# The opening of a banded attention: order of the parts and row sums, queue of the first maxima, place of the block scales

## The chip, the cores and the metric

One of the cores of a Trainium2 chip runs the whole program. The metric is the device time of one execution in microseconds, taken over several runs.

## The reference, cut to what matters

Four layers are added to a stream x of 16 batches x 128 rows x 512 columns (float32): an attention over the columns within a band of 64, a feed-forward net whose three weights go through a 4-bit round trip (NF4), a cross attention, and a mixture of experts. The change touches only the time in which the first of them runs, and with it the round trip of the feed-forward weights, which is computed beside it.

```
x = x + _L0_xattn_ref(_layernorm(x), ctx_2048, ...)   # band |i - j| <= 64, 8 heads of 16
x = x + _L0_ffn_ref(_layernorm(x), weight1, weight2, weight3)
# nf4 round trip of each weight, in blocks of 64 values:
scalers_1 = max(abs(blocks), axis=1); scaler_mean = scalers_1.mean()
centered = scalers_1 - scaler_mean; sb = centered.reshape(nsb, 64)
qf = 256 / (2 * max(abs(sb), axis=1)); q_scalers = clip(round(sb * qf), -128, 127)
idx = argmin(abs(blocks / scalers_1 - NF4)); w = NF4[idx] * (q_scalers / qf + scaler_mean)
```

## The kernel before, in words

`phase_layer0_attention` is written out by hand: each engine has its own program, and semaphores tie them together. A batch is one 128 x 512 tile of x. It is normalised (`norm_x`), multiplied by the query and key weights (`proj`, TensorE, into two PSUM banks), and each product is split into three bf16 parts that add up to the float32 value: `first_part` and `second_part` on ScalarE, `resid_part` and `third_part` on VectorE. The parts have one SBUF buffer for all batches. SyncE writes it to DRAM (`write_parts`, L245) and loads it back in another order as the stacks `q_stack` and `k_stack` (`load_stack`, L253; twelve transfers for a batch, six for each half of the heads), which have two buffers. `first_part` of a later batch therefore waits until the write of the earlier one has landed.

The scores are computed twice. A first pass (`smax`, L508) gives the products of a half of the heads, in eight chunks, whose row maxima VectorE takes with the band mask (`take_max`, L777). The maxima are turned by TensorE (`max_t`, L514), split into two bf16 parts (`max_parts`, L789 and L791), written to DRAM and loaded back as two more rows of `q_stack` (`max_out` and `max_back`, L257 and L261, on SyncE). The second pass (`scores`, L523 and L528) then includes them, so that ScalarE can take the exponential directly (`exps`, L386). For the very first half (batch 0, first heads) GpSimd does this write and read, L334 and L336, with semaphores of their own; the scores of batch 0 wait for `s_mr0`. The two PSUM banks of the first pass alternate, and one of them also takes the turned maxima: from the second round on, TensorE's sixth chunk waits for `max_parts`.

```
def max_out(b, g, u):
    sp.wait_ge(s_mp, 2 * u + 2)
    sp.dma_start(dr_max[2 * b + g]..., mparts[:]).then_inc(s_mw, 16)
...
if c == MT_AT + 2:
    pe.wait_ge(s_mp, 4 * i + 6)
smax(2 * i + 3, 1 - b, 1, c)
```

In the main loop (`batches`; batches 0, 1 and the last two are written out, the others are a hardware loop) a batch has two rounds of eight chunks c. In each chunk TensorE does one first-pass chunk of the next half, one second-pass chunk of this half, a piece of the summing of the quantised weights (`nf4_sum`, L574), and here and there a product with the attention's values (`pv`, L540), a turn of outputs (L548, L554), a projection. VectorE does the maxima of a chunk and between them the pieces of the NF4 round trip.

The round trip needs block scales. For weight 1 the absolute maxima of the blocks of 64 are taken in the opening (L876), for weights 2 and 3 from magnitudes that ScalarE computes during batch 0 (`magnitudes`, `block_max`). GpSimd writes them to DRAM and reads them in another order (`gather_maxima`, L311 and L314); VectorE sums them and takes reciprocals (`block_sums`, `block_recip`, L850, L844, L845), TensorE forms the mean (L583), VectorE computes the scales in eleven dependent steps (`block_mean` L855, `block_scales`, L863 to L873), and GpSimd writes and reads them once more (`spread_scales`, L318 and L322). `nf4_weight` (L919) needs them: for the first two chunks of the weights those of weight 1, from the third on those of weights 2 and 3 as well. That third chunk is at the start of batch 2, the first turn of the hardware loop.

GpSimd's queue holds, in this order: load of weight 1, three loads of x, the gathering for weight 1, the first maxima's write and read, a wait for the first half of batch 1's stacks (`s_ld[0]` at 192), the loads of weights 2 and 3 (L306), the spreading of weight 1's scales. ScalarE's opening holds the parts of batch 0 (L364, L368), a root for two batches, four row sums (`row_sum`, L414: batches 4 to 7), the parts of batch 1, eight more row sums, twelve square sums (L419), the root of all of them (L440), then the main loop with the normalising of batch 2 (L373).

Of the kernel before, what the change touches and what calls it, by code (L numbers as in the profile page):

```python
# [25 lines left out]
NB, S, D = 16, 128, 512  # L26
# [50 lines left out]
def phase_layer0_attention(nc, T, I):  # L77
# [13 lines left out]
    DVE_ROWS = 4  # L91
# [15 lines left out]
    qst = sb("q_stack", [P, 2, H0, D], BF16)  # L107
# [3 lines left out]
    mparts = sb("max_parts", [16, 2, P], BF16)  # L111
# [41 lines left out]
    dr_max = nc.dram_tensor("dr_max", [4, 2, 16, P], BF16).ap()  # L153
# [73 lines left out]
    with nc.Block() as block:  # L227

        @block.sync
        def _(sp):  # L230
# [34 lines left out]
            for i in range(2):  # L265
                write_parts(i, i)
                for g in range(2):
                    load_stack(i, i, g, 16)
            def body(j, i, b, first, last, final):
                max_out(b, 1, 2 * i + 1)  # L270
                max_back(b, 1, 2 * i + 1)
                ge(sp, s_y, i - 1)
                sp.dma_start(ctx_sb[:, b, :], I["ctx"][bass.ds(i, 1), :, :].rearrange("o p d -> p (o d)")).then_inc(s_ctx[b], 16)
                if not last:
                    write_parts(i + 2, b)
                if not last:
                    sp.wait_ge(s_s, 16 * i + 8)
                    load_stack(i + 2, b, 0, 8 * (i - b) + 32)
                if not final:
                    max_out(1 - b, 0, 2 * i + 2)  # L280
                    max_back(1 - b, 0, 2 * i + 2)
                if not last:
                    sp.wait_ge(s_s, 16 * i + 16)
                    load_stack(i + 2, b, 1, 8 * (i - b) + 32)
# [4 lines left out]
        def _(pool):  # L289
# [40 lines left out]
            pool.memset(kst[96:98].rearrange("p a h t -> p (a h t)").bitcast(F32), TWO_ONES).then_inc(s_ko, 1)  # L330
            pool.wait_ge(s_am, 1)
            gather_maxima(0, 1)
            pool.wait_ge(s_mp, 2)
            pool.dma_start(dr_max[0].rearrange("c a t -> a c t"), mparts[:]).then_inc(s_mw0, 16)  # L334
            pool.wait_ge(s_mw0, 16)
            pool.dma_start(qst[96:98, 0, 0:4, :], dr_max[0].rearrange("c (h q) t -> c h (q t)", h=4)).then_inc(s_mr0, 16)  # L336
            pool.wait_ge(s_ld[0], 192)
            load_nf(1)
            load_nf(2)
# [8 lines left out]
        def _(act):  # L348
# [74 lines left out]
            for k in range(2):  # L423
                second_part(0, k)
            root(2, DVE_ROWS)
            for b in range(DVE_ROWS, DVE_ROWS + 4):
                row_sum(b)
            for k in range(2):
                first_part(1, 1, k)
            for k in range(2):  # L430
                second_part(1, k)
            for b in range(DVE_ROWS + 4, NB):
                row_sum(b)
            act.wait_ge(s_rs1, NSUM)
            act.activation(negmean[:, DVE_ROWS:NB], rsum[:, DVE_ROWS:NB], ACT.Copy, scale=-1.0 / D).then_inc(s_rs1, 1)
# [279 lines left out]
        def _(dve):  # L715
# [209 lines left out]
            def body(j, i, b, first, last, final):  # L925
                second = isinstance(i, int) and i == 1
                for c in range(8):
                    if not final:
                        take_max(2 * i + 2, 0, c)
                    if c in (3, 4) and not last:  # L930
                        resid_part(i + 2, c - 3)
                    if c == MT_AT:
                        max_parts(2 * i + 1, MT)
                    if c == 5 and not final:
                        v_copy(i + 1, 1 - b)
                    if c == 7 and first:
                        block_max(0)
                    if c == 5 and first:
                        block_scales(0, 1)
                    if c == 5 and second:  # L940
                        block_sums(1, 3)
                        block_recip(1, 3)
                    if c in (6, 7) and not last:
                        third_part(i + 2, c - 6)
                    if c == 7 and not first:
                        o_norm(i - 1, 1)
                    if c == 0:
                        if not first:
                            nf4_weight(2 * i - 2)
                    nf4_compare(2 * i, 0, c)  # L950
                    if c == 2:
                        nf4_scale(2 * i + 1, 1)
                for c in range(8):
                    if not final:
                        take_max(2 * i + 3, 1, c)
                        if c == MT_AT:
                            max_parts(2 * i + 2, MT)
                    if c == 2 and second:
                        block_mean(1, 3)
                    if c == 3 and second:  # L960
                        block_scales(1, 3)
                    if c in (1, 4, 7) and first:
                        block_max(1 + c // 3)
                    if c == 6 and not first:
                        gated(i - 1, 1 - b)
                    if c == 7:
                        o_norm(i, 0)
                    if c == 0:
                        if not first:
                            nf4_weight(2 * i - 1)  # L970
                    nf4_compare(2 * i + 1, 1, c)
                    if c == 2:
                        nf4_scale(2 * i + 2, 0)
                if first:
                    row_scale(2, DVE_ROWS, NB)
                if not first:
                    add_x(i - 1)
# [1929 lines left out]
```

## Time and profile before

| | us |
|---|---|
| three runs, median (lowest to highest) | 1455.07 (1453.42 to 1456.38) |
| profiled execution, its own time | 1452.38 |
| span of that execution | 1450.6 |
| start of the first scores product | 45.2 |

Times in the rows are microseconds from the span's start. "PE" is TensorE, "DVE" VectorE, "ACT" ScalarE, "POOL" GpSimd, "SPq" the issuing of SyncE. In the timeline a row gives start, duration, engine, line, operation, output and inputs, and in brackets the idle time of the engine before it with what ended it. L508 is line 508 of the program.

### The profile page before, as it was taken

To read this page: it belongs to the slowest core of one execution; us is meant where nothing else is said; L and a number is where in the kernel's file an instruction comes from. 1 tells how busy PE (TensorE), PEld (TensorE's weight loads), DVE (VectorE), ACT (ScalarE), POOL (GpSimd) and SP (SyncE) were. 2 spreads that over 40 slices of the span, in tenths; PEclk is the share of its full clock that TensorE was granted. 3 is DMA by queue.
4 is the path that set the end of the run, shared out by engine and by line. 5 is a ranking of instruction groups with operands and counts; after the bars stand their busy time and mean duration, and the time that the engine had idled before them with its cause. 6 is when DMAs were issued, how large, how long until landed. Compare 5 with 4: busy or idle time off the path is not lost. (4 is left out here: it accounts for less than half of the span.)

```text
span 1450.6 us, 28759 instructions
## 1 busy us (share of the span) xinstructions
PE 1355.9 (93%) x8732; PEld 818.1 (56%) x8732; DVE 977.6 (67%) x3234; ACT 788.2 (54%) x1802; POOL 245.7 (17%) x265
## 2 busy tenths in 40 slices
PE   3688999999999899999989999998788999999998
PEld 1345656565555444444455555555434877777774
DVE  6988999999996545546456788777568655444211
ACT  4877888888878533332367666667420233333231
POOL 3100000000000100000011000013311255555452
PEclk7799999999999999999999999999999999999999
DMA  8634353434430400000020000000413588898885
GB/s 258 172 79 99 81 123 96 117 95 111 108 82 10 146 0 0 0 0 1 0 76 15 16 16 14 14 0 31 151 70 111 165 259 251 246 255 251 243 243 116
DMA packets 63186, 149.52 MB, mean 103 GB/s; under 512 B 10792, under 2 KB 27830, under 8 KB 58892
## 3 DMA queue, kind: packets, MB, share of 16 engines
q1 hardware_dynamic: 49836, 115.70, 26.4%
q0 software_dynamic: 13280, 32.93, 9.9%
q8 instruction: 38, 0.62, 0.2%
q14 instruction: 32, 0.26, 0.1%
HBM read 113.21 MB, written 35.39 MB: 102 GB/s over the span
## 5 line engine op out<-in xcount | busy, mean ns | idle before, releaser
L777 DVE CUSTOM_DVE_ANT_0 masked_scores<-ps_max,band_mask 128x192 bf16<-128x192 f32 (+1 forms) x512 | 176.7, 382 | 17.7 <-PE ps_max L508 12.8
L386 ACT ACTIVATE probs_t<-ps_sc 128x448 f32<-128x448 f32 x256 | 139.1, 544 | 67.8 <-PE ps_sc L528 67.7
L1256 PE MATMUL f_ps<-f_xt,w_t 128*128 (+1 forms) x704 | 160.2, 382 | 2.5 <-ACT w_t L1311 2.5
L380 ACT ACTIVATE nf_above<-nf_scaled,nf_sign_at 128x512 f16<-128x512 bf16 x231 | 161.9, 717 | 0.0
L2804 DVE TENSOR_TENSOR d_inter<-d_silu_g,d_su 128x384 f32<-128x384 f32 x32 | 17.7, 554 | 161.7 <-PE d_su L2488 156.4
L1928 ACT ACTIVATE c_probs<-d_sg,c_negmax 128x128 f32<-128x128 f32 x256 | 90.3, 365 | 58.3 <-DVE c_negmax L2013 57.9
L508 PE MATMUL ps_max<-k_stack,q_stack 96*128 96x192 bf16 (+1 forms) x512 | 95.9, 271 | 26.7 <-DMA k_stack<-dr_parts 12.7
L1256 PEld LDWEIGHTS f_ps<-f_xt,w_t 128*128 128x128 bf16 x704 | 69.3, 98 | 86.7 <-issue 4.9
L2321 POOL DMA_INDIRECT out<-d_h,d_scatter_now x64 | 97.3, 1520 | 107.2 <-DMA out<-d_h,d_scatter_now 90.4
L2672 DVE TENSOR_SCALAR d_onehot<-d_slot_no,d_pos 128x192 bf16<-128x192 bf16 x512 | 101.0, 288 | 0.3 <-PE d_lb L2389 0.3
L508 PEld LDWEIGHTS ps_max<-k_stack,q_stack 96*128 96x128 bf16 x512 | 45.7, 100 | 93.8 <-issue 64.0
L2482 PE MATMUL d_su<-d_h,d_wgu 128*128 128x192 f32 x512 | 93.8, 338 | 1.4 <-DVE d_h L2791 1.1
L523 PE MATMUL ps_sc<-band_mask,identb 128*128 128x448 bf16 x256 | 92.0, 359 | 1.7 <-ACT probs_t L386 1.7
L528 PE MATMUL ps_sc<-q_stack,k_stack 98*128 98x192 bf16 (+1 forms) x512 | 92.5, 262 | 0.0
L2482 PEld LDWEIGHTS d_su<-d_h,d_wgu 128*128 128x128 f32 x512 | 84.5, 194 | 9.8 <-issue 9.8
L2488 PE MATMUL d_su<-d_h,d_wgu 128*128 128x192 f32 x512 | 88.7, 326 | 0.8 <-issue 0.8
L2488 PEld LDWEIGHTS d_su<-d_h,d_wgu 128*128 128x128 f32 x512 | 84.0, 190 | 1.1 <-issue 1.1
L1430 DVE SCALAR_TENSOR_TENSOR f_h<-f_ps,f_h_scale,f_silu 128x512 f32<-128x512 f32 x44 | 32.9, 749 | 76.7 <-PE f_ps L1256 76.6
L2013 DVE TENSOR_REDUCE c_negmax<-d_sg 128x4 f32<-128x512 f32 x64 | 44.1, 688 | 50.7 <-PE d_sg L1706 50.0
L1337 ACT ACTIVATE f_hparts<-f_h 128x512 f16<-128x512 f32 x44 | 27.7, 630 | 86.5 <-DVE f_h L1430 86.5
L2587 ACT ACTIVATE d_h<-d_sg 128x384 f32<-128x384 f32 (+1 forms) x32 | 14.0, 437 | 98.4 <-PE d_sg L2469 56.6
L528 PEld LDWEIGHTS ps_sc<-q_stack,k_stack 98*128 98x128 bf16 x512 | 50.9, 99 | 27.7 <-issue 2.2
(385 smaller groups left out, 2869.3 us busy)
## 6 DMA issues: line engine op xcount, KB each, us to landing
d_wgu<-in_ex_gu SPq DMA_DIRECT2D x32, 1024.0 KB, 6.9
d_wdown<-in_ex_d SPq DMA_DIRECT2D x32, 512.0 KB, 6.1
dr_parts<-qk_parts SPq DMA_DIRECT2D x32, 384.0 KB, 4.9
q_stack<-dr_parts SPq DMA_DIRECT2D x32, 192.0 KB, 2.8
k_stack<-dr_parts SPq DMA_DIRECT2D x32, 192.0 KB, 3.4
out<-x_sb SPq DMA_DIRECT2D x21, 256.0 KB, 2.1
nf_w<-in_nf_w POOLq DMA_DIRECT2D x3, 1408.0 KB, 9.3
q_stack<-dr_parts SPq DMA_DIRECT2D x32, 128.0 KB, 2.4
```

What stands on the lines that cost most here:

```text
L380: act.activation(above[:, g, k, :], lvl[:, g, :], ACT.Sign, bias=cut[:, k - NDV:k - NDV + 1]).then_inc(s_sg, 1)
L386: act.activation(pt[:, c, :], SP[c % 2][:].rearrange("p a w -> p (a w)")[:, a:z], ACT.Exp, scale=D0 ** -0.5).then_inc(s_e, 1)
L508: mm = pe.matmul(m[:, k, off:off + hi - lo], qst[0:96, b, h, qt * P:qt * P + P], kst[0:96, b, h, lo:hi], start=True, stop=True)
L523: pe.matmul(s[:].rearrange("p a w -> p (a w)")[:, a:z], identb[:], mask[:].rearrange("p a w -> p (a w)")[:, a:z], start=True, stop=False)
L528: mm = pe.matmul(s[:, k, off:off + hi - lo], kst[0:98, b, h, kt * P:(kt + 1) * P], qst[0:98, b, h, lo:hi], start=False, stop=(k == 1))
L777: op = dve.tensor_tensor_reduce(masked[:, c % 2, k, off:off + hi - lo], M[c % 2][:, k, off:off + hi - lo], mask[:, k, off:off + hi - lo], ...
L1256: mm = pe.matmul(bank[:], w12[:, m, kt, ft * P:(ft + 1) * P], xt[:, q, kt, bass.ds(g * N, N)], start=(kt == 0 and q == 0), stop=(kt == KT ...
L1928: op = act.activation(pr[:, ot % 2, j, :], SB[ot % 2][:, j, :], ACT.Exp, bias=nm[:, ot % 2, j:j + 1], accum_out=sm[:, bb, 4 * ot + j:4 * o ...
L2321: pool.indirect_dma_start(out, bass.IndirectOffsetOnAxis(ap=sst[rows_of[a], par, a:a + 1], axis=0), yo[a][:, par, :], None, compute_op=ALU ...
L2482: mm = pe.matmul(GP[:, it, :], wg[:, par, t, it * P:(it + 1) * P], xt[:, par, t, :], start=(t == 0), stop=(t == KT - 1))
L2488: mm = pe.matmul(UP[:, it, :], wg[:, par, t, FI + it * P:FI + (it + 1) * P], xt[:, par, t, :], start=(t == 0), stop=(t == KT - 1))
L2672: op = dve.tensor_scalar(oh[:, half, tl, jj, :], ios[:], pos[:, half * HT + tl, bass.ds(4 * q + jj, 1)], None, ALU.is_equal)
```

## The change

ScalarE's opening: the parts of batch 1 come ahead of all twelve row sums, where four of them stood ahead before. The first maxima are written and read by SyncE, behind the twelve issues of batch 1's stacks, and no longer by GpSimd; the semaphores are the same. In batch 1's rounds, VectorE's sums and reciprocals for weights 2 and 3 move from chunk 5 to chunk 4 of the first round, and the scales of these weights from chunk 3 to chunk 2 of the second round, where they follow the mean directly.

```diff
--- before.py
+++ after.py
@@ -266,6 +266,11 @@
                 write_parts(i, i)
                 for g in range(2):
                     load_stack(i, i, g, 16)
+            sp.wait_ge(s_mp, 2)
+            sp.dma_start(dr_max[0].rearrange("c a t -> a c t"), mparts[:]).then_inc(s_mw0, 16)
+            sp.wait_ge(s_mw0, 16)
+            sp.dma_start(qst[96:98, 0, 0:4, :], dr_max[0].rearrange("c (h q) t -> c h (q t)", h=4)).then_inc(s_mr0, 16)
+
             def body(j, i, b, first, last, final):
                 max_out(b, 1, 2 * i + 1)
                 max_back(b, 1, 2 * i + 1)
@@ -330,10 +335,6 @@
             pool.memset(kst[96:98].rearrange("p a h t -> p (a h t)").bitcast(F32), TWO_ONES).then_inc(s_ko, 1)
             pool.wait_ge(s_am, 1)
             gather_maxima(0, 1)
-            pool.wait_ge(s_mp, 2)
-            pool.dma_start(dr_max[0].rearrange("c a t -> a c t"), mparts[:]).then_inc(s_mw0, 16)
-            pool.wait_ge(s_mw0, 16)
-            pool.dma_start(qst[96:98, 0, 0:4, :], dr_max[0].rearrange("c (h q) t -> c h (q t)", h=4)).then_inc(s_mr0, 16)
             pool.wait_ge(s_ld[0], 192)
             load_nf(1)
             load_nf(2)
@@ -423,13 +424,11 @@
             for k in range(2):
                 second_part(0, k)
             root(2, DVE_ROWS)
-            for b in range(DVE_ROWS, DVE_ROWS + 4):
-                row_sum(b)
             for k in range(2):
                 first_part(1, 1, k)
             for k in range(2):
                 second_part(1, k)
-            for b in range(DVE_ROWS + 4, NB):
+            for b in range(DVE_ROWS, NB):
                 row_sum(b)
             act.wait_ge(s_rs1, NSUM)
             act.activation(negmean[:, DVE_ROWS:NB], rsum[:, DVE_ROWS:NB], ACT.Copy, scale=-1.0 / D).then_inc(s_rs1, 1)
@@ -937,7 +936,7 @@
                         block_max(0)
                     if c == 5 and first:
                         block_scales(0, 1)
-                    if c == 5 and second:
+                    if c == 4 and second:
                         block_sums(1, 3)
                         block_recip(1, 3)
                     if c in (6, 7) and not last:
@@ -957,7 +956,7 @@
                             max_parts(2 * i + 2, MT)
                     if c == 2 and second:
                         block_mean(1, 3)
-                    if c == 3 and second:
+                    if c == 2 and second:
                         block_scales(1, 3)
                     if c in (1, 4, 7) and first:
                         block_max(1 + c // 3)
```

## Rows read from the trace of the kernel before

**Rows 1.** The profile's page: busy time, share of the span and instructions of each engine.

```profile
PE 1355.9 (93%) x8732; PEld 818.1 (56%) x8732; DVE 977.6 (67%) x3234; ACT 788.2 (54%) x1802; POOL 245.7 (17%) x265
```

**Rows 2.** The timeline of all engines, the opening up to 40 us.

```profile
16.91 0.63 ACT L414 ACTIVATE unread<-x_sb 128x512 bf16<-128x512 f32 x1 [3.14 <-DMA x_sb<-in_x]
...
25.25 1.26 ACT L364 ACTIVATE qk_parts<-ps_g,bias 128x512 bf16<-128x512 f32 x2 [5.78 <-DMA dr_parts<-qk_parts]
...
30.68 0.90 PE L508 MATMUL ps_max<-k_stack,q_stack 96*128 96x192 bf16 x4 [12.74 <-DMA k_stack<-dr_parts]
...
38.49 0.56 POOL L334 DMA_DIRECT2D dr_max<-max_parts  x1 [11.80 <-DVE max_parts L791]
...
39.13 1.35 SPq L253 DMA_DIRECT2D k_stack<-dr_parts  x3
```

**Rows 3.** The timeline of all engines, 40 to 62 us.

```profile
41.81 0.30 ACT L440 ACTIVATE std<-square_sum,eps 128x12 f32<-128x12 f32 x1
...
42.99 1.90 POOL L306 DMA_DIRECT2D nf_w<-in_nf_w  x2
...
45.11 1.28 ACT L386 ACT_TABLE_LOAD   x1
45.23 0.58 PE L523 MATMUL ps_sc<-band_mask,identb 128*128 128x448 bf16 x1
...
49.66 0.42 DVE L777 CUSTOM_DVE_ANT_0 masked_scores<-ps_max,band_mask 128x256 bf16<-128x256 f32 x1 [1.31 <-PE ps_max L508]
```

**Rows 4.** The timeline of TensorE, 60 to 132 us.

```profile
60.47 0.48 PE L508 MATMUL ps_max<-k_stack,q_stack 96*128 96x192 bf16 x2 [3.50 <-DVE row_max L777]
...
97.02 0.32 PE L508 MATMUL ps_max<-k_stack,q_stack 96*128 96x192 bf16 x2 [0.89 <-DVE row_max L777]
...
105.17 0.38 PE L508 MATMUL ps_max<-k_stack,q_stack 96*128 96x256 bf16 x2
...
109.61 0.39 PE L508 MATMUL ps_max<-k_stack,q_stack 96*128 96x256 bf16 x2 [2.35 <-DVE row_max L777]
...
113.38 0.35 PE L523 MATMUL ps_sc<-band_mask,identb 128*128 128x448 bf16 x1
...
118.98 0.59 PE L574 MATMUL ps_nf<-nf_above,ident_f 128*128 128x512 f16 x2 [1.89 <-DVE nf_w L919]
```

**Rows 5.** The timeline of VectorE, 86 to 122 us.

```profile
94.08 0.40 DVE L850 TENSOR_REDUCE sc_sums<-sc_blocks 88x2 f32<-88x256 bf16 x1
...
94.67 1.25 DVE L845 RECIPROCAL absmax_recip<-absmax_recip 128x176 f32<-128x176 f32 x1
...
102.52 0.15 DVE L855 TENSOR_SCALAR sc_mean<-ps_g 128x2 bf16<-128x2 f32 x1
...
104.79 0.40 DVE L863 TENSOR_TENSOR sc_bf<-sc_blocks,sc_mean 88x256 bf16<-88x256 bf16 x1
...
108.17 0.42 DVE L873 TENSOR_TENSOR sc_bf<-sc_bf,sc_mean 88x256 bf16<-88x256 bf16 x1
...
118.14 0.69 DVE L919 SCALAR_TENSOR_TENSOR nf_w<-ps_nf,block_scale 128x512 f32 x1 [2.32 <-DMA block_scale<-dr_rep]
```

**Rows 6.** Groups by line, 0 to 60 us: busy us, mean ns, idle before.

```profile
L414 ACT ACTIVATE unread<-x_sb 128x512 bf16<-128x512 f32 x12 | 7.4, 615 | 3.1 <-DMA x_sb<-in_x 3.1
```

**Rows 7.** DMA issues, 0 to 60 us: queue, count, KB each, median us to landing.

```profile
sc_blocks<-dr_sc POOLq DMA_DIRECT2D x1, 22.0 KB, 5.0
...
dr_max<-max_parts POOLq DMA_DIRECT2D x1, 8.0 KB, 3.7
q_stack<-dr_max POOLq DMA_DIRECT2D x1, 8.0 KB, 2.0
dr_max<-max_parts SPq DMA_DIRECT2D x1, 8.0 KB, 2.8
```

**Rows 8.** The source line L257 (SyncE's maxima writes), 0 to 130 us.

```profile
DMA to landing us min/median/max: 1.4/2.1/3.3
```

**Rows 9.** Busy us by window: PE, PEld, DVE, ACT, POOL, then granted clock, DMA share, GB/s.

```profile
60.00:64.00 4.00, 3.53 (x26) 1.69 (x26) 3.90 (x12) 2.78 (x6) 1.57 (x2) 0.57 0.08 8
```

## The prediction

> **What bounds the kernel now.** Read the shares first: TensorE is busy 93% of the span, VectorE 67%, ScalarE 54% [rows 1]. That average does not hold in the first 120 us, the only part that the change touches. The timeline of the opening is read next, following who waits for whom. TensorE's first score product starts at 30.68 after 12.74 us of waiting for the k stack's load from DRAM; the load, in turn, waits for the parts of batch 0 to be written. ScalarE has finished four row sums by 19.5 (they start at 16.91 when x arrives), then sits idle 5.78 us and starts the parts of batch 1 at 25.25, released by the landing of the write of batch 0's parts, whose buffer it reuses [rows 2]. So the row sums do not hold the parts back; a transfer does. From 45 us on TensorE and VectorE alternate as the bound: at 49.66 VectorE had waited 1.31 us for TensorE, at 60.47 TensorE 3.50 us for VectorE [rows 3, 4]. Nothing between them is timed by anything outside, so a shift at 45 us should travel to the end. The one exception in this stretch is at 118.14, where VectorE stood 2.32 us for the block scales of weights 2 and 3, a transfer, and TensorE in its wake 1.89 us until 118.98 [rows 4, 5].
>
> **The change part by part.** (1) *Row sums behind the second batch's parts.* Gain: none, since the parts wait for the landing at 25.25 either way. Price: four of twelve sums leave an idle gap and enter a queue that is full afterwards: 4 x 0.615 = 2.5 us [rows 6]. The last root then moves from 41.81 to 44.3 and ends at 44.6; the normalising of batch 2 and the table load at 45.11 follow it 0.3 us later. The first exponential needs the scores, whose first product is at 45.23 and takes about 1 us; with 45.11 + 0.3 + 1.3 for the load ScalarE is ready at 46.7 [rows 3]. If part (2) delays the scores as below, this is covered; if it does not, up to 0.3 us remain. I take 0.
>
> (2) *First maxima on SyncE's queue.* Removed from GpSimd: two issues and two waits. GpSimd issued the write at 38.49, and it landed 3.7 us later; the read then landed 2.0 us after its own issue, near 44.4, ahead of the product at 45.23 that needs it [rows 2, 3, 7]. On SyncE both stand behind all issues of batch 1's stacks. The last group of three starts at 39.13 and takes 1.35 us, so the queue is free at 40.5: 2.0 us later than GpSimd was [rows 2]. For the landing from this queue the nearest rows are the same 8 KB transfer later on: 1.4 at best, 3.3 at most, and 2.8 for the one within the first 60 us [rows 7, 8]. I take 2.8, as this write leaves directly behind twelve stack loads: it lands at 43.3. The read starts at 43.4. GpSimd meanwhile is no longer held up by the maxima. It waits only for the first half of batch 1's stacks, whose issues end near 37.7 (two groups of 1.4 us before 39.13), and with some 3.5 us to land it issues the loads of weights 2 and 3 near 41 in place of 42.99 [rows 3]. So the read runs beside that traffic; again 2.8, landing at 46.2. The scores start 0.9 us late. The bounds: 40.5 + 1.4 + 2.0 = 43.9, in time, cost 0; or 40.5 + 3.3 + 5.0 = 48.8, cost 3.6, with the 5.0 us of the small load that ran beside stack loads [rows 7]. Because TensorE is the one that is waited for up to 49.66, all of it passes on to VectorE [rows 3]. What is queued behind SyncE's new waits is only the next maxima, which come from the main loop's fourth chunk: 0. The weights' earlier arrival feeds magnitudes that ScalarE takes only in its sixth: 0.
>
> The Trainium skill, "DMA: Bandwidth & Descriptors", section "Two DMAs through the same engine are not ordered", says that within one queue descriptors start in order: a rule against this move, as the maxima now start behind the stacks. By it alone, the write could not beat the last stack load, and the sum would stay as it is; no row isolates it.
>
> (3) *Block scales one chunk sooner, their sums one chunk sooner.* The sums and reciprocals run from 94.08 to 95.9 [rows 5]; a chunk earlier they delay the v copy by 1.9 us, which TensorE needs to turn the outputs. TensorE had 0.89 us of waiting for VectorE before 97.02 [rows 4], so about 1 us could come out; VectorE sets the pace up to 109.61, where TensorE waits 2.35 us for it. I take 0, bounded by 1. The chain of scales itself moves from 104.79 to right behind the mean, 102.52 + 0.15 = 102.67: 2.1 us earlier. It takes 108.17 + 0.42 - 104.79 = 3.8 us [rows 5]. The block scales would then land near 116.0 instead of 118.1. But the chain now stands ahead of the fourth maxima and the maxima's parts, so those end near 108.6 and not 104.8. TensorE's sixth chunk (105.17) reuses the bank that the parts are read from and waits for them. So the idle time moves from before 109.61 to before 108.6, and the 2.1 us of work between 105.17 and 107.26 come after it: the seventh chunk starts at 110.7 instead of 109.61, 1.1 us late. The work up to the stall ended at 118.98 - 1.89 = 117.1; it now ends at 118.2, and no scale is missing any more. Gain 118.98 - 118.2 = 0.8 us. Bounds: at most the whole 1.9 of TensorE's stall (if the bank is not what holds TensorE). At the other end the maxima for batch 2's first half, ready at 108.6 rather than 104.8, need a write and a read of 1.4 to 3.3 each [rows 8], so arrive between 111.4 and 115.2, and are due at 113.38 + 1.1 = 114.5 [rows 4]: a loss of up to 0.7 that takes the gain.
>
> **Sum.** +0.9 (2) +0 (1) -0.8 (3) = +0.1 us against the profiled execution's 1452.38, that is 1452.5. That execution ran 2.7 us below the median of three, 1455.07, so the forecast for a median is 1455.1. A measurement of this kernel tells about 0.2%, or 2.9 us, from no change; of the bounds only the 3.6 us of part (2) leaves it.
>
> **Rivals.** *A: the maxima are in time.* If the write lands 1.4 us after issue and the read like GpSimd's 2.0, the scores are not delayed, and the late gain stands alone, 0.8 to 1.9 us: 1453.2 to 1454.3, call it 1453.7. For it: the median of five such writes is 2.1 us [rows 8]. Against it: this one stands behind twelve loads, and the slower ones of the five are what traffic makes of them. The Trainium skill, same page, section "Latency and other measured facts", gives about 0.6 us to the first byte for a hardware queue and about 1 us for GpSimd's. By that the two transfers would save some 0.8 us of the 2.0 us lost in the queue, an estimate between A and my forecast. Chance 0.25.
>
> *B: slower, through the read.* The weights' traffic starts before the read, which takes 5.0 us. It decides from a landing after 45.23; at 48.8 it costs 3.6, less 0.8: 1457.9. For it: small loads beside large ones took up to 5.0 us [rows 7]. Against: the stacks drain by then, and the read has only 8 KB. Chance 0.14.
>
> *C: the clock.* In 60 to 64 us the granted clock was 0.57 of full on average, i.e. mostly at 1.2 GHz, just after TensorE's idle 3.50 us [rows 4, 9]; 4 x (1 - 0.57) = 1.7 us of full-speed work. Part (3) merges the waiting into one gap of 3.4 us (105.2 to 108.6). If the clock falls after it, 1.7 is lost where 0.8 was to be won: 1455.07 + 0.1 + 1.7 = 1456.9. The Trainium skill, "TensorE: Matmul & The Clock Gate", section on oscillation, warns of idle gaps that cost the full clock; the trace agrees at 60 us. Chance 0.15. The forecast has 0.46.
>
> **Numbers.** The range goes from A's lower end less the spread of the runs (1453.2 - 0.9) to B: 1452.3 to 1457.9. Faster by over 0.2% needs 1452.2: A plus a clock fall that goes away, 0.08. Slower by over 0.2% needs 1458.0: B or C with the bounds of the others, 0.11. Same 0.81.
>
> **What would show it.** (1) Batch 1's parts again near 25.3, the last root 2.5 us later. (2) The write of the first maxima at 40.5, the first scores between 45.2 and 48.8, GpSimd's weight loads near 41. (3) No wait of VectorE for the block scales near 118; a gap of about 3.4 us on TensorE before 108.6; the clock after it decides C. I am wrong if the parts of batch 1 start before 24, which would mean that ScalarE did not wait for the landing, or if the late stall stays.

## The result: 0.3 to 0.4% slower, and the profile after

| | us | ratio to before (95% interval) |
|---|---|---|
| before, median of 8 runs (lowest to highest) | 1452.60 (1449.07 to 1456.38) | |
| changed, median of 8 | 1458.95 (1456.03 to 1460.97) | 1.0044 (1.0031 to 1.0056) |
| changed, second time, 9 runs | 1455.76 (before then 1453.75) | 1.0028 (1.0014 to 1.0041) |
| changed, third time, 7 runs | 1457.57 (before then 1452.11) | 1.0038 (1.0024 to 1.0052) |

The ratios, here and in the table of the experiments, are not the quotient of the two medians beside them and differ from it by up to 0.0014 (the medians of the second time give 1.0014). Where the text below gives a distance in us, it is worked out from the ratio, or it names the median.

The profiled execution of the changed kernel took 1459.27 us (span 1457.5), 6.9 us more than that of before. I had forecast 1455.1, not to be told from no change ("Same 0.81"), in a range of 1452.3 to 1457.9. The measured 1458.95 lies above the range. The forecast started from a median of three, 1455.07. With eight runs the median of before is 1452.60, so the measured distance to before is 6.4 us where 0.1 was forecast. The page's shares hardly differ (columns: busy us, share, instructions), but the first two slices of the granted clock do (tenths of full speed; before it began with 7, 7, 9):

```profile
PE 1358.1 (93%) x8732; PEld 818.9 (56%) x8732; DVE 978.7 (67%) x3234; ACT 788.9 (54%) x1802; POOL 244.8 (17%) x263
...
PEclk7689999999999999999999999999999999999999
```

The opening, in the timeline of all engines (start, duration, engine, line, operation; in brackets the idle time before). These rows answer to [rows 2]:

```profile
25.39 1.27 ACT L365 ACTIVATE qk_parts<-ps_g,bias 128x512 bf16<-128x512 f32 x2 [11.52 <-DMA dr_parts<-qk_parts]
...
31.25 0.90 PE L507 MATMUL ps_max<-k_stack,q_stack 96*128 96x192 bf16 x4 [12.74 <-DMA k_stack<-dr_parts]
...
39.90 1.35 SPq L253 DMA_DIRECT2D k_stack<-dr_parts  x3
...
41.30 0.42 SPq L270 DMA_DIRECT2D dr_max<-max_parts  x1
...
41.57 1.89 POOL L311 DMA_DIRECT2D nf_w<-in_nf_w  x2 [14.74 <-DMA k_stack<-dr_parts]
...
44.41 0.30 ACT L439 ACTIVATE std<-square_sum,eps 128x12 f32<-128x12 f32 x1
```

ScalarE's parts of batch 1 start at 25.39, as before, released by the landing of batch 0's write; the idle time ahead of them is longer, since no row sums stand in it. SyncE issues the last stack group at 39.90 and the write of the maxima at 41.30. GpSimd, no longer held, issues the weights at 41.57. The next stretch of the same view, to be read against [rows 3]:

```profile
45.40 0.27 SPq L272 DMA_DIRECT2D q_stack<-dr_max  x1
...
45.69 1.28 ACT L387 ACT_TABLE_LOAD   x1
...
50.53 0.56 PE L522 MATMUL ps_sc<-band_mask,identb 128*128 128x448 bf16 x1 [4.53 <-DMA q_stack<-dr_max]
...
51.50 0.54 ACT L387 ACTIVATE probs_t<-ps_sc 128x448 f32<-128x448 f32 x1 [4.53 <-PE ps_sc L527]
...
52.07 0.42 DVE L776 CUSTOM_DVE_ANT_0 masked_scores<-ps_max,band_mask 128x256 bf16<-128x256 f32 x1 [4.23 <-PE ps_max L507]
```

The write landed 4.1 us after its issue: the read leaves at 45.40. The first scores product starts at 50.53, after 4.53 us of waiting for this read, which took 5.1 us for 8 KB. ScalarE's table was loaded by 47.0 and it waited 4.53 us too; VectorE 4.23. What filled that time, by windows of 1 us (columns: length, TensorE busy and instructions, granted clock, DMA share, GB/s):

```profile
44.00:45.00 1.00, 0.00 (x0) 0.50 1.03 256
...
46.00:47.00 1.00, 0.01 (x1) 0.50 1.08 365
...
49.00:50.00 1.00, 0.00 (x0) 0.50 0.99 369
...
51.00:52.00 1.00, 1.00 (x6) 0.50 1.00 394
52.00:53.00 1.00, 1.00 (x4) 0.50 0.11 39
...
54.00:55.00 1.00, 1.00 (x5) 0.50 0.00 0
...
56.00:57.00 1.00, 1.00 (x9) 1.00 0.00 0
```

From 45 to 52 the DMA engines moved 336 to 400 GB/s, the weights, and were fully busy (share about 1); they ran empty just after 52. TensorE did nothing from 46 to 50.5 and had the low clock until 55.6, where before it had risen at 50. Further on, TensorE's timeline in two stretches, against [rows 4]:

```profile
65.92 0.48 PE L507 MATMUL ps_max<-k_stack,q_stack 96*128 96x192 bf16 x2 [3.50 <-DVE row_max L776]
```

```profile
104.26 0.65 PE L547 MATMUL ps_g<-ident,o_cols 128*128 128x128 f32 x4 [1.61 <-DVE v_ones L762]
...
116.67 0.39 PE L507 MATMUL ps_max<-k_stack,q_stack 96*128 96x256 bf16 x2 [3.32 <-DVE max_parts L790]
...
127.53 0.59 PE L573 MATMUL ps_nf<-nf_above,ident_f 128*128 128x512 f16 x2
```

The 3.50 us gap of batch 0 is there again, 5.45 us later. The v copy is waited for (1.61 us at 104.26), and the gap ahead of the sixth chunk is 3.32 us. VectorE, against [rows 5]:

```profile
110.71 0.42 DVE L862 TENSOR_TENSOR sc_bf<-sc_blocks,sc_mean 88x256 bf16<-88x256 bf16 x1
...
114.12 0.42 DVE L872 TENSOR_TENSOR sc_bf<-sc_bf,sc_mean 88x256 bf16<-88x256 bf16 x1
...
126.35 0.69 DVE L918 SCALAR_TENSOR_TENSOR nf_w<-ps_nf,block_scale 128x512 f32 x1
```

The chain of scales follows the mean directly and ends at 114.5; the third weight chunk (126.35) waits for nothing. The stall is cured. The clock in three stretches (columns after the length: TensorE, its loads, VectorE, ScalarE, GpSimd busy; clock; DMA share; GB/s):

```profile
74.00:84.00 10.00, 8.04 (x45) 3.88 (x46) 8.60 (x35) 6.93 (x10) 0.00 (x0) 0.66 0.37 100
...
89.00:97.00 8.00, 6.37 (x17) 3.01 (x18) 5.13 (x24) 5.12 (x9) 2.65 (x3) 0.57 0.16 14
116.00:121.00 5.00, 4.33 (x29) 2.00 (x30) 2.98 (x16) 1.15 (x2) 1.91 (x2) 0.66 0.22 21
```

These stretches take in some 7, 7 and 3.4 us at 1.2 GHz; before had 3.4 us in each of the corresponding first two (the stretch of [rows 9] lies ahead of them), and none at the third. Where the difference arises, from the two timelines:

| start of | before | changed | late by |
|---|---|---|---|
| first-pass product of batch 0 | 30.68 | 31.25 | 0.6 |
| first scores product | 45.23 | 50.53 | 5.3 |
| second round of batch 0 | 60.47 | 65.92 | 5.5 |
| projection after batch 0 | 83.72 | 90.63 | 6.9 |
| third weight chunk | 118.14 | 126.35 | 8.2 |
| end of the span | 1450.6 | 1457.5 | 6.9 |

So 4.7 us are the new wait, 0.6 is a later start that differs between profiles of one kernel (30.4 to 31.3 in the three of the changed one), and the growth from 5.3 to 8.2 lies in batches 0 and 1, where the clock differs. The growth is not a fixed part of the change: in the two later profiles of the changed kernel (r1, r3) the scores start 4.0 and 3.6 us late and the third weight chunk 3.8 and 3.7.

### The profile page after: what moved, and what is told of

Same layout as the page of the kernel before. It is cut to its first block and busy times, and to the rows that moved or that the text cites. A ratio compares the mean times of both kernels' runs of the same rounds, so it can differ in the third digit from the quotient of the medians.

```text
span 1457.5 us, 28759 instructions
## 1 busy us (share of the span) xinstructions
PE 1358.1 (93%) x8732; PEld 818.9 (56%) x8732; DVE 978.7 (67%) x3234; ACT 788.9 (54%) x1802; POOL 244.8 (17%) x263
```

## The experiments

All were timed in five rounds beside the kernel before. "Third chunk" is the start of the third weight chunk (VectorE, `nf4_weight`) in the profile. In the profiles of before, of the change and of every experiment without fillers or a moved spreading, the execution's time less this start was 1332 to 1337 us, so that the differences that the profiles can explain lie ahead of it.

One profile was taken of each, of one execution, and equal kernels differ there: it places the waits, and the runs give the time.

| | median (before) | ratio (95%) | first scores | third chunk |
|---|---|---|---|---|
| e4 sums only | 1451.56 (1451.74) | 1.0001 (0.9988 to 1.0014) | 45.23 | 117.6 |
| e3 scales and block sums | 1452.69 (1451.74) | 1.0004 (0.9990 to 1.0018) | 45.53 | 118.2 |
| e8 scales without block sums | 1453.80 (1453.49) | 1.0005 (0.9994 to 1.0015) | 45.87 | 118.1 |
| e2 change without queue move | 1453.99 (1451.74) | 1.0016 (1.0001 to 1.0030) | 44.81 | 118.7 |
| e1 queue move only | 1455.05 (1451.74) | 1.0021 (1.0004 to 1.0038) | 49.19 | 124.5 |
| r2 queue move only, again | 1456.99 (1452.11) | 1.0026 (1.0012 to 1.0041) | 49.04 | 125.0 |
| e14 change without scales | 1455.78 (1452.11) | 1.0031 (1.0017 to 1.0046) | 49.49 | 122.1 |
| e13 queue move, weights held | 1451.62 (1452.11) | 1.0003 (0.9990 to 1.0016) | 46.50 | 117.9 |
| e5 change, weights held | 1453.87 (1453.49) | 0.9998 (0.9988 to 1.0007) | 46.38 | 122.6 |
| e6 change, maxima between halves | 1454.82 (1453.49) | 1.0009 (0.9996 to 1.0022) | 45.78 | 120.3 |
| e7 both of these | 1453.12 (1453.49) | 0.9995 (0.9983 to 1.0008) | 45.91 | 121.9 |
| e12 scales, gap filled | 1456.30 (1453.75) | 1.0025 (1.0009 to 1.0041) | 46.20 | 120.7 |
| e10 spreading on SyncE | 1451.20 (1453.75) | 0.9991 (0.9979 to 1.0002) | 45.28 | 120.6 |
| e11 that, and batch 0's gap filled | 1458.87 (1453.75) | 1.0034 (1.0020 to 1.0048) | 45.78 | 117.4 |

### Which part: e1, e2, e3, e4

**e1: the queue move alone**, on the kernel before.

```diff
+            sp.wait_ge(s_mp, 2)
+            sp.dma_start(dr_max[0].rearrange("c a t -> a c t"), mparts[:]).then_inc(s_mw0, 16)
+            sp.wait_ge(s_mw0, 16)
+            sp.dma_start(qst[96:98, 0, 0:4, :], dr_max[0].rearrange("c (h q) t -> c h (q t)", h=4)).then_inc(s_mr0, 16)
...
-            pool.wait_ge(s_mp, 2)
-            pool.dma_start(dr_max[0].rearrange("c a t -> a c t"), mparts[:]).then_inc(s_mw0, 16)
-            pool.wait_ge(s_mw0, 16)
-            pool.dma_start(qst[96:98, 0, 0:4, :], dr_max[0].rearrange("c (h q) t -> c h (q t)", h=4)).then_inc(s_mr0, 16)
```

> The kernel before with the first maxima on SyncE's queue, and nothing else of the change. If the move of the maxima carries the loss (theory M: first scores at 50.5 instead of 45.2 in the changed kernel, 4.7 us of it beyond the common drift), this kernel shows the first scores near 50 and is 4.5 to 6.5 us slower than before. If the loss is shared with the scales' place or with the clock after it (rival P), it is only 1 to 3 us slower.

The timeline of e1:

```profile
40.97 1.89 POOL L311 DMA_DIRECT2D nf_w<-in_nf_w  x2 [13.26 <-DMA k_stack<-dr_parts]
...
44.28 0.27 SPq L272 DMA_DIRECT2D q_stack<-dr_max  x1
...
49.19 0.55 PE L524 MATMUL ps_sc<-band_mask,identb 128*128 128x448 bf16 x1 [3.75 <-DMA q_stack<-dr_max]
```

Here, too, the weights go out ahead of the read, and the read takes 4.9 us. The first scores are 4.0 us later than before. The median is 3.3 us above, between the 1 to 3 us of one theory and the 4.5 to 6.5 of the other, with an interval of 0.6 to 5.5 us: it did not separate them, hence r2 below.

**e2: the change with the maxima on GpSimd.**

```diff
-            sp.wait_ge(s_mp, 2)
...
             gather_maxima(0, 1)
+            pool.wait_ge(s_mp, 2)
...
```

> The changed kernel with the first maxima back on GpSimd's queue; row sums and block scales stay moved. Theory M: first scores back near 45.3, and the time within 1.5 us of before. Rival P: still 3 us or more slower than before, with TensorE at the low clock after its gap in batch 1.

The scores are back at 44.81. The time is 2.3 us above before (0.1 to 4.4): larger than the 1.5 us that theory M allowed, not the 3 of the rival. Undecided.

**e3: only the scales' part.**

```diff
-                    if c == 5 and second:
+                    if c == 4 and second:
                         block_sums(1, 3)
                         block_recip(1, 3)
-                    if c == 3 and second:
+                    if c == 2 and second:
                         block_scales(1, 3)
```

> The kernel before with only the block sums and block scales moved one chunk ahead. My reckoning: 0.8 us faster if the clock stays, 1 us slower if it falls after the 3.4 us gap; theory M takes the first, rival P wants 2 us or more slower here.

No change that can be measured: 0.6 us, with an interval of -1.5 to 2.6. The third chunk starts where it did (118.2 against 118.1) although the stall is gone. Why, the granted clock shows. First e3, its gap in TensorE's timeline and the window behind it; then the same window of the kernel before:

```profile
107.24 0.61 PE L508 MATMUL ps_max<-k_stack,q_stack 96*128 96x256 bf16 x2 [3.33 <-DVE max_parts L791]
```

```profile
106.00:114.00 8.00, 6.76 (x38) 3.46 (x39) 4.77 (x23) 2.31 (x4) 2.06 (x3) 0.57 0.15 15
```

```profile
106.00:114.00 8.00, 5.65 (x47) 3.25 (x46) 7.62 (x31) 4.71 (x9) 2.65 (x3) 1.00 0.34 63
```

The window from 106 to 114 had 0.57 of the clock in e3 and all of it in the kernel before.

**e4: only the row sums.**

```diff
-            for b in range(DVE_ROWS, DVE_ROWS + 4):
-                row_sum(b)
...
-            for b in range(DVE_ROWS + 4, NB):
+            for b in range(DVE_ROWS, NB):
                 row_sum(b)
```

> The kernel before with only the four row sums moved behind the second batch's parts. Both theories: the parts start at 25.3 as before, the last root moves from 41.8 to 44.3, the first exponential is at most 0.3 us late; time within 0.5 us of before.

As expected: 1.0001, scores at 45.23. The last root came at 44.84, 3.0 us later and not 2.5; it cost nothing.

### Traffic or place in the queue: e5, e6, e7

**e5: the weights' loads wait for the maxima.**

```diff
             pool.wait_ge(s_ld[0], 192)
+            pool.wait_ge(s_mr0, 16)
             load_nf(1)
```

> The changed kernel, but GpSimd issues the loads of weights 2 and 3 only after the first maxima are back in the query stack. Theory T (the read is slow because it runs beside the weights' loads): the read takes about 2 us instead of 5.1, first scores near 47.5 (the write still leaves at 41.3 and takes about 4), 3 us faster than the changed kernel. Rival Q (the place in SyncE's queue and its own slowness cost the time): the read stays above 4 us, and less than 1 us is won.

```profile
41.12 0.42 SPq L270 DMA_DIRECT2D dr_max<-max_parts  x1
...
44.88 0.27 SPq L272 DMA_DIRECT2D q_stack<-dr_max  x1
...
46.38 0.56 PE L523 MATMUL ps_sc<-band_mask,identb 128*128 128x448 bf16 x1 [0.44 <-DMA q_stack<-dr_max]
...
46.90 1.89 POOL L311 DMA_DIRECT2D nf_w<-in_nf_w  x2 [19.09 <-DMA q_stack<-dr_max]
```

The write leaves as late as in the changed kernel (41.12) and takes 3.8 us, but the read is in after 1.5 us instead of 5.1. The first scores come at 46.38 (1.1 us sooner than expected, 4.1 sooner than in the change), and the time is that of before. The queue's place still costs a little: TensorE waits 0.44 us.

**e6: the maxima between the halves of the stacks** (SyncE's four lines stand there and no longer behind), weights as in the change.

```diff
                 for g in range(2):
+                    if (i, g) == (1, 1):
+                        sp.wait_ge(s_mp, 2)
...
                     load_stack(i, i, g, 16)
```

> The changed kernel, but SyncE writes and reads the first maxima between the two halves of the second batch's stacks, so that they no longer stand behind the second half. The weights' loads are as in the changed kernel. Theory T and rival Q agree that the write leaves near 38.7 instead of 41.3. T: write and read are done by 44 before the weights' traffic is under way, scores at 45.3, and 4 to 5 us faster than the changed kernel. If only the traffic's start counts and it falls on the read anyway, 2 us are won.

```profile
38.78 0.32 SPq L270 DMA_DIRECT2D dr_max<-max_parts  x1
...
41.19 0.27 SPq L272 DMA_DIRECT2D q_stack<-dr_max  x1
41.29 1.88 POOL L311 DMA_DIRECT2D nf_w<-in_nf_w  x2 [13.36 <-DMA k_stack<-dr_parts]
...
45.78 0.58 PE L522 MATMUL ps_sc<-band_mask,identb 128*128 128x448 bf16 x1
```

The read goes out 0.1 us ahead of the weights and nobody waits for it. The scores start at 45.78 with no wait, as foretold; the time is 1.3 us above before (-0.6 to 3.2), so that most of the change's 4.1 to 6.4 us came back; whether the 4 us that were expected did, the intervals do not tell.

**e7: both.**

```diff
+                    if (i, g) == (1, 1):
+                        sp.wait_ge(s_mp, 2)
...
+            pool.wait_ge(s_mr0, 16)
```

> Both: maxima between the halves of the stacks, and weights only after they are back. Expected: maxima in place near 42.5, first scores at 45.3, bound by the maxima of the second half; time as without the queue move at all, that is within 1.5 us of before.

As expected: 0.9995. Row sums and scales are moved in e5 and e7 and cost nothing measurable there (upper ends of the intervals: 1.0 and 1.2 us), which speaks against the 2.3 us of e2. In e7 the read took 2.0 us (issued at 41.48, and the weights' loads, which waited for it, at 43.50) beside the stack loads of the second half.

### The sums' chunk and the clock: e8, e12

**e8: the scales earlier, the block sums where they were.**

```diff
-                    if c == 3 and second:
+                    if c == 2 and second:
                         block_scales(1, 3)
```

> The kernel before with only the block scales one chunk ahead; the block sums stay at their chunk. If the v copy's delay (TensorE waited 1.61 us for it in the changed kernel) costs time by itself, this kernel is 0.5 to 1.5 us faster than the one with both moved; if it is absorbed by TensorE's later wait, they are equal within 0.5 us.

1.0005 against e3's 1.0004. The intervals of some 2 us to either side are too wide to tell 0.5 us from 1.5, and the equal third chunks (118.1 and 118.2) prove little, since the low clock behind the gap lasted 3.4 us in e8 and 6.8 in e3. What does show it is VectorE's time from the second residual of this round (`qk_resid`, at 91.23 in e8 and 90.24 in e3) to the end of TensorE's gap (108.36 and 107.24): 17.1 us without the moved sums and 17.0 with them. TensorE's wait for the v copy, 1.61 us in e3 and missing in e8, is absorbed before the gap ends.

**e12: e3 with the gap filled.**

```diff
                         if c == MT_AT + 2:
+                            if isinstance(i, int) and i == 1:
+                                pe.wait_ge(s_e, 8 * (2 * i + 1) + c - 1)
+                                for _ in range(14):
+                                    pe.matmul(SP[c % 2]..., identb[:], mask[:]..., start=True, stop=True)
                             pe.wait_ge(s_mp, 4 * i + 6)
```

> The kernel before with block sums and scales one chunk ahead, and the new 3.3 us gap ahead of the sixth chunk of batch 1 filled in the same way. Theory C: the scales-only kernel had the low clock from 106.7 to 113.9 after this gap and gained nothing; with the gap filled the clock stays up, the third weight chunk starts near 116 and not 118.2, and the kernel is 1 to 2 us faster than the scales-only one. If the clock does not matter, it starts at 118 as there.

```profile
109.08 3.18 PE L667 MATMUL ps_sc<-band_mask,identb 128*128 128x512 bf16 x14
112.53 0.39 PE L508 MATMUL ps_max<-k_stack,q_stack 96*128 96x256 bf16 x2 [0.27 <-DVE max_parts L795]
```

```profile
106.00:114.00 8.00, 7.73 (x48) 3.92 (x50) 7.59 (x33) 4.41 (x9) 1.63 (x2) 1.00 0.63 158
```

With 3.18 us of products in the gap TensorE waited 0.27 us, and the clock stayed at full. From this chunk to the third weight chunk it took 8.1 us (112.53 to 120.66), in e3 11.0 (107.24 to 118.19). In this stretch the fallen clock had cost 2.8 us. As a whole e12 was slower than before, 1.0025, and not 1 to 2 us faster than e3. Its profile came to the third chunk late (120.7, low clock earlier on) and took 1339 us behind it instead of 1332 to 1337; but this execution, 1459.95 us, was itself 3.7 us above e12's median, so it does not place the loss.

All profiles with the moved scales, and those without that had the clock up there, can be set beside each other (us; the low clock is the time at 1.2 GHz between the sixth chunk and the third weight chunk):

| kernels, low clock | profiles | sixth chunk to third weight chunk | second to third weight chunk |
|---|---|---|---|
| moved scales, none | e12 | 8.1 | 17.1 |
| moved scales, 3.4 | changed, e5, e7, e8 | 9.7 | 18.6 to 18.7 |
| moved scales, 6.8 | r1, r3, e2, e3, e6 | 10.9 to 11.1 | 19.9 to 20.0 |
| scales not moved, none | before, e4, e13, e14, r2 | | 17.9 to 18.4 |

So each 3.4 us at the low clock cost 1.3 to 1.6 us. With the clock up the stretch from the second chunk was 0.8 to 1.4 us shorter than in the kernels that kept the stall, near the forecast 0.8. With the low clock it was 0.2 to 2.1 us longer than theirs, in all nine profiles.

### The late stall cured otherwise: e10, e11

**e10: SyncE spreads the scales of weights 2 and 3**, with semaphores of its own.

```diff
-            pool.wait_ge(s_sc, 2)
-            spread_scales(1, 3)
...
                     max_back(1 - b, 0, 2 * i + 2)
+                if isinstance(i, int) and i == 1:
+                    sp.wait_ge(s_sc, 2)
+                    spread_scales(1, 3)
```

> The kernel before with another cure for the late stall: the scales stay where they were, but their write and reads (weights 2 and 3) go over SyncE's queue, which is idle then, in place of GpSimd's. If the stall at 118 is the transfer alone, the reads land before 115.8, VectorE's 2.3 us wait and TensorE's 1.9 us wait are gone, no new gap appears ahead of the sixth chunk, and the third weight chunk starts near 116.2: 1 to 2 us faster than before.

SyncE's timeline:

```profile
112.32 0.30 SPq L257 DMA_DIRECT2D dr_rep<-sc_bf  x1
113.84 1.10 SPq L261 DMA_DIRECT2D block_scale<-dr_rep  x2
116.73 1.26 SPq L254 DMA_DIRECT2D q_stack<-dr_parts  x3
```

Write and reads fit ahead of the stacks of batch 3, and neither VectorE nor TensorE has a wait for the scales any more. From the second to the third weight chunk it took 17.4 us (before: 99.73 to 118.14, 18.4) in spite of 3.4 us at the low clock from 112.6. This does not yet speak for the cure: e1, which left the spreading on GpSimd, also had 3.4 us of low clock there, no wait for the scales, and 17.4 us (the last section shows why). The median is 2.6 us below before, the ratio 0.9991 with 1.0002 in its interval: not shown to be faster. The profiled execution was the slowest of its twelve (1457.86 us).

**e11: e10, and batch 0's 3.5 us gap filled.**

```diff
+                    if c == 0 and first:
+                        for _ in range(14):
+                            pe.matmul(NF[:], identb[:], mask[:]..., start=True, stop=True)
```

> The one before, and TensorE's 3.5 us gap in batch 0 (57 to 60.4) filled with 14 products of 512 columns into a bank that is free then; their results are never read. If the idle gap is what takes the clock to 1.2 GHz (theory C), the low stretch at 60 to 64 is gone and up to 1.7 us more are won; if the clock falls all the same, nothing is won, and if the filler overruns the gap, up to 1 us is lost.

```profile
56.61 3.18 PE L668 MATMUL ps_nf<-band_mask,identb 128*128 128x512 bf16 x14
60.27 0.33 PE L518 MATMUL ps_max<-k_stack,q_stack 96*128 96x192 bf16 x2 [0.48 <-DVE row_max L790]
```

The gap shrank to 0.48 us and the low stretch at 60 to 64 is gone, as theory C wanted; the clock fell at 69 instead, in a wait of 2.08 us. The third chunk came at 117.4, and 16.0 us after the second. Those 16.0 us, with the clock up and no wait for the scales, are nearly 2 us less than in any kernel with the stall and the clock up: here the cure shows. But the kernel is slower, 1.0034: behind the third chunk the profile has 1342 us, with more low clock between 1300 and 1400 us (granted clock 0.97 there, 1.00 before). That is not the whole reason: three of its seven executions had a mean granted clock of 0.978 and took 1456.4 to 1459.7 us, while 24 executions of the kernel before at that clock took 1449.4 to 1456.4. Why fillers in the opening go with a slower kernel stays open.

### The size of each part: r1, e13, r2, e14, r3

**r1, r3: the changed kernel again**, no edit.

> The changed kernel again, beside new runs of the kernel before. In the profiles so far all that separates the kernels is done by the start of the third weight chunk (118.1 before, 126.4 changed, 124.5 with the queue move alone); from there to the end every profile has 1333 to 1335 us. If that describes the executions in general, the ratio is 1.003 to 1.006 again. If the first comparison caught unlucky executions, it is at 1.002 or below, as the queue move alone had.

> The changed kernel beside them: 4 to 6 us slower than before, first scores near 49 to 50.5.

1.0028 is just below the expected 1.003 to 1.006, 1.0038 (5.5 us) within the expected 4 to 6 us; both are clear of 1. The first scores came at 49.24 and 48.85, the read taking 5.0 and 5.3 us.

**e13: the queue move alone, weights held** (e1 with the line of e5).

```diff
+            sp.wait_ge(s_mp, 2)
...
+            pool.wait_ge(s_mr0, 16)
```

> The kernel before with the maxima on SyncE's queue and the weights' loads held until they are back. Theory T (traffic): the read takes about 1.5 us, first scores near 46, and 3 to 4 us faster than the queue move alone, that is within 1.5 us of before. If the place in the queue counts by itself, it stays 2 us or more slower than before.

```profile
44.98 0.27 SPq L272 DMA_DIRECT2D q_stack<-dr_max  x1
...
46.50 0.56 PE L525 MATMUL ps_sc<-band_mask,identb 128*128 128x448 bf16 x1
...
47.02 1.88 POOL L311 DMA_DIRECT2D nf_w<-in_nf_w  x2 [19.00 <-DMA q_stack<-dr_max]
```

1.5 us for the read, the third chunk at 117.9, and the time of before.

**r2: the queue move alone, again**, the edit of e1.

> The queue move alone again. Theory T: first scores near 49.2, 3 to 5 us slower than before. If the low first measurement was right and the loss lies elsewhere, 2 us or less.

1.0026, 3.8 us (1.7 to 6.0; 4.9 by the medians), and the first scores at 49.04: within what theory T expected. Beside e13, its partner with the weights held, it is 3.4 us slower (difference of the means, 95% within 2.1 us of that).

**e14: the change without the scales' part** (e1 with the edit of e4).

```diff
+            sp.wait_ge(s_mp, 2)
...
-            for b in range(DVE_ROWS, DVE_ROWS + 4):
-                row_sum(b)
...
```

> The change without its third part: queue and row sums moved, block sums and scales where they were. If the third part costs nothing, as the reckoning from its profile says (clock loss against the stall it removes), equal to the changed kernel within 1.5 us. If the third part carries 2 us, as the kernel without the queue move hinted, it is faster than the changed kernel by that.

1.0031 against the changed kernel's 1.0038 beside it. The difference is 1.0 us by the ratios and 1.8 by the medians; that of the means is 1.5, with 95% within 1.7 us of it. This leaves the scales' part between nothing and some 3 us.

## Why the prediction was wrong

**The row sums: right.** The parts of batch 1 started at 25.39, and e4 changed nothing (1.0001). The last root came 2.6 us later in the changed kernel and 3.0 in e4, for the 2.5 reckoned.

**The queue move: the right path, a mis-sized term.** The step that failed is "So the read runs beside that traffic; again 2.8, landing at 46.2. The scores start 0.9 us late." The read took 5.1 us and landed at 50.5. The sources of the error, in order: the read 5.1 instead of 2.8 (2.3 us); the write 4.1 instead of 2.8 (1.3); SyncE free at 41.3 instead of 40.5 (0.8, of which 0.6 is the later start). The sum is 4.4 us, against 50.5 - 46.2 = 4.3. (By its own numbers the forecast was 46.2 - 45.23 = 1.0 us late, not 0.9. The 0.9 us that the range allows for the spread of the runs has no row either: the three runs lay 3.0 us apart.) The value of 2.8 was taken from a transfer that left at 53, in the last moments of the same loads, and read as a price for running beside them. It was the wrong row: the nearest in kind, not in load. The small load of 5.0 us beside stack loads was the nearer one, and I had put it at the far bound. Rival B had the mechanism and the size of the read; even its 48.8 was short, since it kept SyncE's free time and gave the write 3.3. Its chance of 0.14 was the mistake in the judgement. That the traffic makes the read slow, and not the queue, e5 and e13 show: same queue, the read issued within 0.7 us of the same time, no weights in flight, 1.5 us. The write is another matter: behind the twelve stack loads it took 3.8 and 3.2 us in e5 and e13 too, and 2.4 and 2.5 between the halves (e6, e7). Its excess over 2.8 is mostly not the weights'.

The size in time follows: 1.0026 (r2), 1.0021 (e1) for the queue move alone, 1.0003 with the weights held. GpSimd's old waits for the maxima did unintended work: they kept 2.8 MB off the DMA engines until the maxima's read was out. The change was a release of these loads, 1.4 us sooner in time and ahead of the read in order. The prediction saw the release (near 41, measured 41.57) and gave the meeting no price beyond 2.8. With the measured terms its sum is 4.7 for part (2) (in r1 and r3 the scores came 4.0 and 3.6 us late), 0 for part (1) and, by e3 and e8, 0.6 to 0.7 for part (3): 5.3 to 5.4 us, against 4.1, 5.5 and 6.4 measured for the changed kernel.

**The scales' move: right in its steps, wrong in its gain.** The gap of 3.4 us ahead of the sixth chunk (3.32 measured), the stall gone, the delayed v copy absorbed (e8): all came as reckoned. The gain of 0.8 us did not come, because rival C did: the clock fell after the gap in all nine profiles that have the moved scales and no filler. Rival C's price of 1.7 us was about right for one stretch of 3.4 us, as in the changed kernel's first profile (9.7 - 8.1 = 1.6). In five of the nine the low clock lasted 6.8 us and cost 2.8 to 3.0. That the clock is what took the gain rests on these lengths and on the one profile of e12; as a time of the whole kernel no run shows it, since e12 was slower for reasons that stay open. It was not a matter of the gap alone: a 2.35 us gap at this place brought the low clock in e1 and e10 and not in the kernel before, e4, e11, e13, r2 and e14. In time the part is near zero, 1.0004 (e3) and 1.0005 (e8), with up to some 2 us of loss inside the intervals. The trace agrees with the warning of the Trainium skill, "TensorE: Matmul & The Clock Gate", section on oscillation, that idle gaps cost the full clock: in the changed kernel it was low from 117.0 to 120.5, right behind the 3.32 us gap that ended at 116.67.

**What the prediction left out** is that the low stretches of batches 0 and 1 vary from execution to execution. The changed kernel's first profile had 7 us low near 76 to 83 where before had 3.4. That is part of the growth from 5.3 to 8.2 us, but the change is not shown to cause it. The same kernel's other two profiles have no growth (third chunks of 126.4, 121.9 and 121.8 in the three), and e5, e7 and e10, whose times are those of before, have the same long stretches. A late start of the scores does not fix the clock either: with the scores at 48.9 to 49.5 it rose at 52.2 (r1, r3), 54.4 (e14), 54.8 (r2) and 55.1 (e1). This variation goes with the spread of all times here: among 127 executions of the kernel before, the 26 with a mean granted clock of 0.980 or more averaged 1450.3 us, the 18 with 0.976 or less 1454.4.

**Open:** e2's 1.0016 is more than its parts (1.0001 and 1.0004); the intervals overlap, and the profile of e2 shows nothing new but 6.8 us of low clock after the gap. What the scales' part costs in time is known only to lie between nothing and some 2 to 3 us. Why an 8 KB read takes 5 us beside the loads (its packets' turn among the others', or the engines' order) no run took apart.

## What to carry to other kernels

Before an engine is relieved of a wait, list what stands behind that wait: here it was the release of large loads, and they met the small transfer on the critical path. Price a small transfer by a row that has the same traffic beside it, and if the only such row is the far bound, give that case the larger chance. And when a chain is moved ahead of something that another engine needs, the same idle time may be gathered into one gap, after which TensorE's clock fell here in nine profiles of nine.

## What the runs showed that was not expected

An 8 KB read on SyncE's queue took 1.5 us with the DMA engines idle (e5, e13) and 4.9 to 5.3 us in six profiles with the weights going at 319 to 406 GB/s, with the stack loads ahead of it on that queue landed or about to. Issued 0.1 us ahead of the same loads (e6) it cost nobody anything. When it landed there the profile does not show, only that nobody waited for it at 45.78. A likely reason, not shown, is that the loads move data only 1.5 to 2 us after GpSimd starts to issue them: issued at 42.99 in the kernel before and at 46.90 in e5, they are first seen on the DMA engines between 44.5 and 45, and from 48.5.

The late stall that part (3) set out to cure looks like the same effect once more. The block scales' reads, 22 KB each on GpSimd's queue, took 5.1 us in the kernel before, where batch 3's stacks were issued 0.55 us after them, and 3.1 us in e1, where the stacks followed only 2 us behind, after a stretch of low clock. First before, then e1:

```profile
111.29 1.91 POOL L322 DMA_DIRECT2D block_scale<-dr_rep  x2 [1.65 <-DMA dr_rep<-sc_bf]
111.84 1.24 SPq L253 DMA_DIRECT2D q_stack<-dr_parts  x3
```

```profile
118.69 1.91 POOL L327 DMA_DIRECT2D block_scale<-dr_rep  x2 [1.67 <-DMA dr_rep<-sc_bf]
...
120.65 1.23 SPq L253 DMA_DIRECT2D q_stack<-dr_parts  x3
```

All five profiles in which the stacks followed 0.5 us behind (before, e4, e13, e14, r2) have reads of 4.8 to 5.2 us and the stall. In the other eleven with the spreading on GpSimd (e1, e12 and the nine with the moved scales) they took 2.9 to 3.1 us, and nobody waited. That the stacks slow the reads was not tested by an edit of its own.

Filling TensorE's gaps with unread products kept the clock up in place (e11, e12), and yet both kernels were slower. In the one profile of each, 2 and 5 us more than elsewhere lie behind the third weight chunk, in work that the fillers do not touch. No run shows why.
